# Reordering the end of the first stage of a three-layer Perceiver kernel: Toeplitz rows, impulse response, and the order of SyncE's stores and loads

## The reference

```
x = x + xattn(layernorm(x), ctx)   # Sim, softmax over 257 rows, attended rows, 4 features @ W_qv
x = x + attn(layernorm(x))         # gate = sigmoid(x@Wg+bg); scan over 32 tokens, 16 states a channel;
                                   # y = scan + xg; layernorm(y) * gamma + beta
x = x + ffn(layernorm(x))          # ternary weights 256->1024->256, squared ReLU, a low-rank part of rank 16
```

## Time and profile before

| | us |
|---|---|
| median of three timed runs | 538.97 |
| the profiled execution's own time | 538.89 |
| its span, first to last instruction | 536.4 |
| PE busy | 479.4 (89%) |
| DVE busy | 419.9 (78%) |
| ACT busy | 359.4 (67%) |
| POOL busy | 343.9 (64%) |
| mean granted TensorE clock | 0.98 of full speed |

### The profile page before, as it was taken

The page is one execution under the profiler, slowest core; times in us unless marked ns, Lnnn a source line. Parts: engine busy times, 40 slices in busy tenths (PEclk is TensorE's granted clock), DMA queues, the critical chain, the costliest instruction groups (busy, mean ns, idle before and its releaser), DMA issues. The chain is left out here.

```text
span 536.4 us, 13420 instructions
## 1 busy us (share of the span) xinstructions
PE 479.4 (89%) x4310; PEld 402.2 (75%) x4310; DVE 419.9 (78%) x1159; ACT 359.4 (67%) x854; POOL 343.9 (64%) x444
## 2 busy tenths in 40 slices
PE   2397799999999999999999996876799999999996
PEld 2275687888887877687787875765588888888885
DVE  1398888888888999999998884457677987988654
ACT  2555578676876767677676766555578768768753
POOL 1377767676775757756756664503578878888653
PEclk9789999999999999999999999998899999999999
DMA  6734445756584555555645568259502022011102
GB/s 206 197 114 149 138 151 160 219 156 217 145 234 136 177 169 139 191 146 139 199 136 144 194 200 178 60 133 218 125 1 79 1 80 79 26 55 39 41 1 78
DMA packets 81316, 70.38 MB, mean 131 GB/s; under 512 B 39760, under 2 KB 64608, under 8 KB 81248
## 3 DMA queue, kind: packets, MB, share of 16 engines
q1 hardware_dynamic: 81248, 69.54, 45.4%
HBM read 56.87 MB, written 12.65 MB: 130 GB/s over the span
## 5 line engine op out<-in xcount | busy, mean ns | idle before, releaser
L1647 POOL TENSOR_TENSOR sq_lo<-scan_x,sq_hi 128x512 fp32r<-128x512 f32 x63 | 82.7, 1313 | 33.6 <-ACT sq_hi L1619 33.6
L705 PE MATMUL turn_ps<-ident,ctxn 128*128 128x128 f32 x512 | 70.3, 282 | 4.4 <-DMA ctxn<-in_ctx 4.4
L933 ACT COPY ctxT<-turn_ps 128x512 f32<-128x512 f32 x128 | 68.2, 583 | 5.4 <-PE turn_ps L705 5.4
L705 PEld LDWEIGHTS turn_ps<-ident,ctxn 128*128 128x128 f32 x512 | 58.2, 144 | 18.0 <-issue 13.2
L1611 ACT ACTIVATE relu<-fc_ps,fc_square 128x512 f32<-128x512 f32 x64 | 43.8, 684 | 31.0 <-PE fc_ps L1545 30.9
L1689 DVE SCALAR_TENSOR_TENSOR scan_x<-fc_ps,relu 128x512 f32<-128x512 f32 x64 | 43.8, 684 | 26.0 <-ACT relu L1611 25.5
L1121 POOL TENSOR_TENSOR hc_lo<-hc_probT,hc_hi 128x256 fp32r<-128x256 f32 x32 | 23.4, 731 | 61.0 <-ACT hc_hi L942 60.9
L1541 PE MATMUL fc_ps<-xn_hi,fc_T 128*128 128x512 f32 x128 | 52.1, 407 | 2.1 <-DVE scan_x L1689 2.1
L1107 POOL TENSOR_TENSOR rstd<-ve,neg_half 128x1 f32<-128x1 f32 x64 | 35.2, 550 | 27.6 <-DVE ve L1331 17.7
L1541 PE MATMUL fc_ps<-xn_lo,fc_T 128*128 128x512 f32 x128 | 51.1, 399 | 0.0
L1113 POOL TENSOR_TENSOR proj_in<-proj_in,below 128x512 f32<-128x512 f32 x31 | 49.3, 1592 | 0.0
(11 more groups left out here) (227 smaller groups left out, 1400.8 us busy)
## 6 DMA issues: line engine op xcount, KB each, us to landing
ctxn<-in_ctx SPq DMA_DIRECT2D x32, 1024.0 KB, 5.5
resid<-in_x SPq DMA_DIRECT2D x32, 128.0 KB, 5.2
ctx_end<-in_ctx SPq DMA_DIRECT2D x32, 128.0 KB
gated_tokens<-gated SPq DMA_DIRECT2D x32, 128.0 KB, 6.2
scan_x<-gated_tokens SPq DMA_DIRECT2D x60, 64.0 KB, 4.9
out<-resid SPq DMA_DIRECT2D x7, 512.0 KB, 3.1
scan_tokens<-scan_x SPq DMA_DIRECT2D x12, 256.0 KB, 5.1
y_in<-scan_tokens SPq DMA_DIRECT2D x4, 512.0 KB, 4.8
```

Source lines behind the costliest of these rows:

```text
L705: mm = pe.transpose(turn_ps[b % 2][:, (c * JT + t) * P:(c * JT + t + 1) * P], ctxn[p][:, b, t, c * P:(c + 1) * P], ident[:, :])
L933: act.copy(ctxT[:, b, :, 0:J - 1], turn_ps[b % 2][:, :].rearrange("p (k j) -> p k j", k=KD)).then_inc(ctxT_copied, 1)
L1647: pool.tensor_tensor(sq_lo[:, m, :], sq[m % SQ], sq_hi[:, m, :].bitcast(F32), ALU.subtract).then_inc(sq_lo_done, 1)
```

## The change

Four edits in the last steps of stage 1.

1. DVE does `impulse_response` in step 30 right after `normalise1(31)` and ahead of the products of group 29, where it stood at the end of the step.
2. The Toeplitz rows of the first half stand later and apart. On ACT, q = 0 comes after `z` in step 32 (it was the step's first instruction) and q = 1 after `hcq_hi` (it was after the side copy). On POOL, q = 2 comes after `rstd2` in step 32 and q = 3 between `hb_lo` and `hcq_lo`; both stood at the end of step 31. The second half stays after step 32.
3. SP issues the second half of piece 0's store after the last group's store, the load of `y_in` and the load of group 31's tokens, where it stood ahead of all three. ACT does the last group's tanh after `y_block(6)`, which was after `y_block(7)`.
4. DVE does `norm_first` before the sums and moments of chunk 1, where it stood after them.

```diff
@@ SP, end of stage 1
                 store_piece(sp, 0, 0, PB // 2, first_stored[0])
-                store_piece(sp, 0, PB // 2, PB // 2, first_stored[1])
                 step(GROUPS + 1, 0, ())
                 sp.wait_ge(first_stored[0], 16 * NB)
                 sp.dma_start(y_in[:, :, :], scan_dram[0:TOK, :]...).then_inc(y_loaded[0], 16)
                 sp.wait_ge(gated_stored[1], 16 * (GROUPS // 2))
                 scan_load(sp, GROUPS - 1, 1)
+                store_piece(sp, 0, PB // 2, PB // 2, first_stored[1])
                 sp.wait_ge(first_stored[1], 16 * NB)
                 sp.dma_start(y_second[:, :, :], ...)
@@ ACT, step
-                    if g == GROUPS:
-                        place_rows(0, 0)
...
-                    if g == GROUPS:
-                        place_rows(1, 0)
...
                                        bias=nmr2[:, 0:1], scale=rstd2[:, 0:1]).then_inc(z_ready, 1)
+                    if g == GROUPS:
+                        place_rows(0, 0)
...
                         act.copy(hcq_hi[:, :, :], hcqT[:, :, :]).then_inc(hcq_hi_ready, 1)
+                    if g == GROUPS:
+                        place_rows(1, 0)
@@ ACT, after the steps
-                for n in range(6, 8):
-                    y_block(n)
+                y_block(6)
                 tanh_gate(GROUPS - 1)
-                for n in range(8, 12):
+                for n in range(7, 12):
                     y_block(n)
@@ POOL
+                def place_high(q, h):
+                    pool.wait_ge(zeroed, FIRST)
+                    pool.wait_ge(windows_loaded[h], 16 * NB)
+                    pool.tensor_copy(*place(q, h)).then_inc(high_placed, 1)
+                    pool.wait_ge(high_placed, 2 * h + q - 1)
...
                         inverse_deviation(rstd2[:, :], ve2[:, :], ve2_done, rstd2_done, g - 1)
+                    if g == GROUPS:
+                        pool.wait_ge(rstd2_done, g - 1)
+                        place_high(2, 0)
...
                         low_part(hb_lo[:, :, :], hbT[:, :, :], hb_hi[:, :, :], hb_hi_ready, hb_lo_ready, g)
+                        if g == GROUPS:
+                            pool.wait_ge(hb_lo_ready, g)
+                            place_high(3, 0)
                         low_part(hcq_lo[:, :, :], hcqT[:, :, :], hcq_hi[:, :, :], hcq_hi_ready, hcq_lo_ready, g)
...
-                    if g >= GROUPS - 1:
-                        h = g - (GROUPS - 1)
-                        pool.wait_ge(zeroed, FIRST)
+                    if g == GROUPS:
                         pool.wait_ge(hcq_lo_ready, g)
-                        pool.wait_ge(windows_loaded[h], 16 * NB)
                         for q in range(2, NB):
-                            pool.tensor_copy(*place(q, h)).then_inc(high_placed, 1)
-                            pool.wait_ge(high_placed, 2 * h + q - 1)
+                            place_high(q, 1)
@@ DVE
-                    dve.wait_ge(zeroed, FIRST)
+                    dve.wait_ge(zeroed, 1)
...
                         normalise1(g + 1, o, g + 1)
+                    if g == GROUPS - 2:
+                        impulse_response()
...
-                    if isinstance(g, int) and g == GROUPS - 2:
-                        impulse_response()
...
                 x_moments(dve, 0)
+                norm_first(dve)
                 y_sums(dve, 1, range(CH))
                 y_moments(dve, 1)
-                norm_first(dve)
```

## The result

The changed kernel took 543.85 us (median of five runs, 543.58 to 545.63) where the kernel before took 539.34 beside it: ratio 1.0081, 95% interval 1.0049 to 1.0113, so 4.4 us more by the ratio. The profiled execution took 543.87 with a span of 541.6; before 538.89 and 536.4. The forecast was 541.9 (+2.95): the direction was right, the amount too small by 1.4 us against the timed runs and by about 2 us against the profiled execution.

What follows compares the result with a forecast made beforehand. SP, last to drain because it is issuing stores, was taken to set stage 3's start; +2.1 for that start and +0.85 for PE's clock gave +2.95 on 538.89, so 541.9 us, range 539.5 to 545.0.

Steps and rivals of the forecast that it cites:

- The seam: Between stages 1 and 3: all engines are released together, so the last one, SP issuing stores, sets stage 3's start.
- DVE's 1.8 us in step 30: Step 30, impulse response moved earlier: DVE stands still 1.8 us waiting for POOL's product.
- The scan at 338.0: Step 32: scan block 0 starts at 338.0 where it was 339.71, from edits 1 and 2 together.
- The second half 8.1 us from first issue to landed: End of stage 1: piece 0's second half takes 8.1 us to land, and only then may `y_second` be issued.
- The turning of `xn` 1.9: Start of stage 3: after PE's long idle, turning `xn` runs at low clock, 1.9 us for 1.06: +0.85.
- Stage 3 starts at 373.3, +2.1: End of stage 1: second half's landing, `y_second` and eight whole stores on SP delay stage 3 from 371.19 to 373.3.
- The first store was to leave at 343.0: SP late in stage 1: first store leaves at 343.0 for 344.11, behind group 30's tokens, which gain only about 1 us.
- the first half landed after 8.1 us: SP's first store of piece 0: 8.1 us from first issue to landed, so `y_in` leaves at 351.1 instead of 354.96.
- (c): Rival, step 30: PE's 2.3 us idle drops its clock, groups 30 and 31 lose another 1.5; 543.6 us, chance 0.18.
- (a): Rival, end of stage 1: gains arrive, runs of 64 floats cost no extra, DVE is last; 537.1 or 536.3, chance 0.06.
- the 1.4 less what is absorbed: Edit 1's cost: the earlier impulse response makes all of groups 31 and 32 1.4 us later.
- (b): Rival, stage 3 start: nearly no change, +0.5 to +1.5, with PE's clock back early; some 540.3 us, chance 0.26.

## Why the prediction was right in direction and short in size

**What was right, with the number.** The seam decides, and SP is last there: by 4.3 us over DVE where I had some 4, though both ended about 2 us later than I had them. DVE's 1.8 us in step 30: 1.80. The scan at 338.0: 337.91, in part by luck, since `z` of step 32 came 0.45 sooner than I had it (331.65 for 332.1) and what stands between took that much longer. The last group's `gated` at 350.0: 349.86. The second half 8.1 us from first issue to landed: 7.98. The eight whole stores 10.05: 9.84. The turning of `xn` 1.9: 1.94. Moving four stores out of SP's way gave back 4.3 us, and SP's order alone gave ratio 1.0084.

**The terms that were mis-sized.** "Stage 3 starts at 373.3, +2.1" was 375.24, +4.05. That is 1.9 us too little: 2.8 us arose that I did not have, and 0.8 was absorbed behind, most of it where the last tokens would have been waited for anyway. The 2.8 come in two parts, in the sentence on SP's first store and the one after it. The first store was to leave at 343.0 and left at 343.94. Group 30's tokens stand ahead of it: their store took from 338.30 to 342.17, 3.9 us, where it took 1.7 before (339.02 to 340.75), and the loads behind it took 1.73 to issue for 3.16, which gave 1.4 of that back. In the fourteen profiles this landing takes either 1.7 to 2.0 us (seven) or 3.0 to 4.1 (seven); what decides it stays open. And I had the first half landed after 8.1 us, `y_in` out at 351.1; it was 9.94 and 353.88. The 8.1 is not wrong in general: it was 8.0 to 8.6 in four experiments. Its bounds, 7 to 9.5, were given for the second half only and not for the first, which stands in the same chain; that is where the range was laid too narrow. With a first half of 8.2 us, in the changed kernel with the impulse response back, stage 3 starts at 372.86. What made this one execution's first half slow stays open: its fourth transfer took 7.3 us and the second half's fourth 5.4.

**Smaller points.** I expected no PE wait ahead of block 12; it was 2.40 (3.23 before), by the same 2 us that the loads were late. PE idled 7.84 us, not nearly 10, for the same reason. Behind the turning of `xn` another 0.3 us were lost in stage 3, which the sum did not have: 4.05 + 0.88 + 0.27 = 5.2, the difference of the spans. `norm_first` ahead of chunk 1 was forecast as worth nothing; the drains agree, with SP 4.3 us behind DVE, but no run has that edit alone. And the time, 543.85, lies outside the 540.9 to 542.9 to which I gave a half, and next to (c)'s 543.6, although in the profile (c) did not happen: that the range held it does not confirm the sum.

**Rivals.** (a), gains that arrive, fell: stores of neighbouring partitions cost what the rows said, and the estimate by the Trainium skill's price in "DMA: Bandwidth & Descriptors", Anatomy of one DMA (3.2 us for 512 KB) is far from the 8.0 measured; the page fits that price to transfers that GpSimd issues, and these are SP's. Its condition was mistaken too: I put the slowness down to runs of 64 floats. Whole stores have the same runs, and 1 MB of them landed in 8.4 to 9.6 us; every other partition brought 8.0 for 512 KB down to 5.1. It is how a half's batches lie. The Trainium skill has a rule that fits ("SBUF — State Buffer", Door 1: The DMA port swizzle): bandwidth goes by the number of memory ports that the partitions reach, and 0 to 15 reach four where 0 to 31 reach eight. The runs agree, as far as they go: they show that spacing matters, and not that it is the ports. (c), the clock falling in step 30, was real, though not in this profile: it happened in three of seven such profiles, where I gave it 0.18. Its size was right: in the two of the three that have the Toeplitz rows spread as well, the scan starts at 339.75 and 339.44, no sooner than before (339.71) but for 0.3 us. So it isn't a rival to the forecast but a term of it with a probability, and edit 1 costs 2.2 us in the median by itself and some 1.6 within the change (with overlapping intervals), not the 1.4 less what is absorbed that I had. (b) fell.

## What to carry to other kernels

Where a block ends with all engines waiting for each other, look at which one drains last, and count the issuing of transfers as work: an early load bought by a late store is paid for by whoever stands behind the store on the same queue. Before splitting a store to get its first part sooner, look at how long the part takes: a half of neighbouring partitions landed no sooner than the whole, and a half of every other partition in 5.1 to 5.9 us. A wait put on an engine that another needs at full clock can cost more than itself, in some executions and not in others, so time such an edit over several runs.

## What the runs showed of the hardware that I had not expected

- 16 neighbouring partitions of each quarter of 32: 512 KB landed 8.0 to 9.9 us after the first issue; 1 MB from all 32 in 8.4 to 9.6; 512 KB from every second partition in 5.1, and in at most 5.9 (one execution).
- The same idle of 2.7 us of PE left the clock at the high level in four profiles and brought the low one in three. The wait of 2.6 us ahead of the low-rank matmuls in stage 3 did so too: the first of them took 0.47 or 0.48 us in four profiles and 0.76 or 0.77 in eight. At the start of stage 3, after an idle of 7.8 to 8.7 us, it was low in all three profiles that had one (the turning of `xn` took 1.94 us); after 4.1 us the turning took 1.56, after 1.9 us 1.33, and after 0.7 to 1.5 us 1.06 or 1.07.
- How long SP takes to issue a transfer hangs on what it has issued just before: `y_in` took 0.39 us in the changed kernel and 1.74 before, where eight stores stand ahead of it. Of the eight whole stores of 256 KB the first took 0.55 us, and all eight 9.84, which is 1.23 each on average.
